# A graph layer's attention contracts gathered source rows (at most 512 a head) in place of all 1354

## The reference

```python
def _gat_head(h, node_adj, edge_adj, W, a):       # three heads, summed
    hW = h @ W
    hp = (node_adj > 0).astype(hW.dtype) @ hW
    hm = (node_adj < 0).astype(hW.dtype) @ hW
    e_plus = leaky_relu(concatenate([hp, hm], axis=1) @ a, ALPHA)[:, 0]
    e_minus = leaky_relu(concatenate([hm, hp], axis=1) @ a, ALPHA)[:, 0]
    att = where(edge_adj > 0, e_plus[None, :], NEG_INF)
    att = where(edge_adj < 0, e_minus[None, :], att)
    att = softmax(att, axis=1)
    return att * edge_adj @ hW

node_support = node_adj_norm @ h                   # the diagonal is taken out
edge_output = _gru_cell(node_support, h, ...)
node_output = _gru_cell(edge_support, h, ...)      # edge_support: the mean of the three heads
return de[:, None] * edge_output + dn[:, None] * node_output
```

## Time and profile before

| | |
|---|---|
| median of 3 runs | 535.05 us (533.65 to 535.43) |
| span of the profiled execution, first to last instruction | 520.2 us |
| median less span | 14.85 us |
| PE busy | 450.7 us, 87% of the span |
| DVE busy | 342.4 us, 66% |
| ACT busy | 239.3 us, 46% |
| POOL busy | 69.8 us, 13% |
| mean granted clock of PE, as a share of 2.4 GHz | 0.960 |

### The profile page before, as it was taken

How to read it: one execution, slowest core, us unless ns; L and a number is a source line. 1 busy time by engine, 2 the same in 40 slices (tenths; PEclk the granted TensorE clock), 3 DMA queues, 4 the chain that set the end, 5 groups by cost and what they waited for, 6 DMA issues and landing times.

```text
span 520.2 us, 6589 instructions
## 1 busy us (share of the span) xinstructions
PE 450.7 (87%) x1892; PEld 268.2 (52%) x1892; DVE 342.4 (66%) x753; ACT 239.3 (46%) x390; POOL 69.8 (13%) x115
## 2 busy tenths in 40 slices
PE   4588598977698998998979999999988878999996
PEld 2533454544355664454644444444444556787875
DVE  0997979787648772225773887787577655744572
ACT  4987789577777552104134031222213036644441
POOL 5000000000011000000000000100600502564442
PEclk9679788989989999999999999999989999999999
DMA  8889500000000000000000000530100111122422
GB/s 282 275 265 372 238 0 0 0 1 1 0 2 1 0 2 0 1 0 3 1 0 0 1 0 31 184 111 20 45 6 1 48 43 44 53 68 64 123 68 84
DMA packets 27006, 31.70 MB, mean 61 GB/s; under 512 B 3490, under 2 KB 20591, under 8 KB 26967
## 3 DMA queue, kind: packets, MB, share of 16 engines
q1 hardware_dynamic: 25111, 27.71, 16.8%
q0 software_dynamic: 1856, 3.51, 2.0%
HBM read 19.44 MB, written 11.77 MB: 60 GB/s over the span
## 4 chain that ended last, share of the span: by engine, by line
PE 53%; DVE 25%; ACT 11%; issue 9%; POOL 1%; DVEq 0%; POOLq 0%; ACTq 0%
PE bank L1340 9%; PE bank L1149 4%; PE bank L1422 4%; PE bank L1406 4%; PE bank L1288 4%; PE bank L1407 3%; DVE pr_ring L2074 3%; PE bank L1110 2%; DVE y_units L1551 2%; PE bank L1329 2%; DVE y_units L1562 2%; PE bank L999 2%; PE bank L1413 2%; DVE hr_ring L1877 2%; DVE t_units L1557 2%
## 5 line engine op out<-in xcount | busy, mean ns | idle before, releaser
L1340 PE MATMUL bank<-pr_ring,hW 128*128 128x512 f32 (+3 forms) x198 | 94.1, 560 | 6.1 <-DVE pr_ring L2074 5.4
L2074 DVE SCALAR_TENSOR_TENSOR pr_ring<-adjT,regR,bank 128x512 f32<-128x512 f32 (+3 forms) x99 | 64.7, 680 | 35.5 <-PE bank L1329 34.0
L1340 PEld LDWEIGHTS bank<-pr_ring,hW 128*128 128x128 f32 (+1 forms) x198 | 34.4, 193 | 35.3 <-DVE pr_ring L2074 18.4
L999 PE MATMUL bank<-y_units,msg 128*128 128x512 f32 (+3 forms) x66 | 34.4, 652 | 15.1 <-DVE y_units L1572 15.0
L1110 PE MATMUL bank<-hr_ring,W2s 128*128 128x512 f32 (+1 forms) x96 | 45.3, 560 | 0.0
L1877 DVE TENSOR_TENSOR hr_ring<-hr_ring,bank 128x512 f32<-128x512 f32 (+1 forms) x48 | 29.5, 619 | 20.9 <-ACT hr_ring L796 14.9
L585 POOL DMA_INDIRECT yg<-pr_ring,goes x32 | 31.2, 976 | 50.9 <-DVE pr_ring L2113 49.0
L796 ACT ACTIVATE hr_ring<-bank,b1c 128x512 f32<-128x512 f32 (+1 forms) x48 | 29.8, 628 | 15.7 <-PE bank L972 15.7
L970 PE MATMUL bank<-zhi,W1hi 128*128 128x512 f32 (+1 forms) x48 | 35.1, 731 | 0.3 <-DVE zlo L1546 0.3
L2125 DVE TENSOR_TENSOR hbuf<-hbuf,bank 128x341 f32<-128x341 f32 x36 | 18.3, 508 | 23.9 <-PE bank L1407 21.1
L579 POOL DMA_INDIRECT xg<-rowx,slot x22 | 22.3, 1013 | 69.6 <-DVE slot L1684 63.5
(11 more groups left out here) (321 smaller groups left out, 889.9 us busy)
## 6 DMA issues: line engine op xcount, KB each, us to landing
xg<-zeros SPq DMA_DIRECT2D x1, 3575.0 KB
xg<-zeros SPq DMA_DIRECT2D x1, 3055.0 KB
wall<-in_w SPq DMA_DIRECT2D x2, 1364.0 KB
adjT<-in_adjT SPq DMA_DIRECT2D x1, 2560.0 KB
xblk<-xg SPq DMA_DIRECT2D x36, 65.0 KB
adjT<-in_adjT SPq DMA_DIRECT2D x1, 1650.0 KB
adjT<-in_adjT SPq DMA_DIRECT2D x3, 512.0 KB, 5.9
adjT<-in_adjT SPq DMA_DIRECT2D x1, 1024.0 KB
```

The source lines that it names most:

```text
L999: mm = nc.tensor.matmul(B_GNN[:, 0:w], msg[0:r, j, :], y_units[0:r, g % RINGY, i, 0:w], start=(j == 0), stop=(j == T - 1))
L1340: nc.tensor.matmul(B_ACC[:, 0:w], hW[0:r, j, k * P:(k + 1) * P], ring[0:r, 0:w], start=(k == 0 and j == 0), stop=(k == K - 1 and j == T - ...
L2074: nc.vector.scalar_tensor_tensor(out=pr_ring[0:r, 4 + p % R_RING, 0:w], in0=adjT[0:r, j, cols(c)], scalar=g_col[0:r, j, k:k + 1], in1=B_F[ ...
```

## The change

For each head, a source is needed if one of its neighbours (as a destination) has its top bucket at most one bucket above the source's own. The new code finds these sources, numbers them, and makes the loop run over four gathered tiles of 128 sources a head, in place of eleven tiles.

- `onehot_turned` turns the one-hot bucket rows. `reaches` multiplies, for each destination tile, the buckets in reach with the natural adjacency (`nat`, bf16), 33 matmuls in all, and DVE's `reached` masks the sum. `needed`, `needs`, `slots`, `numbered`, `placed`, `payload` and `listed` turn that into up to 512 slots a head and, for each slot, the source's bucket, its factor and its row number (`slot_row`, semaphore `row_set`).
- POOL then issues 36 indirect DMAs, one for each chunk, head and slot tile, from five new DRAM tables. The three tables `near` hold the 512 columns of chunk 0 and the 128 of `hW` of that head; `far1` and `far2` hold the columns of chunks 1 and 2. SP writes them earlier from `adjT` and `hW`, and writes zeros over their diagonals, one element at a time. `nat` is loaded by POOL with a cast, 7.3 MB read.
- The loop has 36 steps (`STEPS`); `numerator` waits for the gathered tiles (`fetched0` to `fetched11`). `spread` now has 12 transposes in all instead of 33.
- The branch on `flag` moves to just ahead of the loop, since it also covers a head that needs over 512 sources. With it, all the edge GRU's tasks (`gates`, `mid`, `new`, `blend`, `add` with n = 0) move out of the loop, ahead of it, where `gates(0, c)` waits for `add(0, c-1)` (`x_edge`).
- The side tasks left get new places in the 36 steps; those of chunk 1's routing stand behind the last step.

With the reference's inputs the three heads need 253, 304 and 421 sources by a count made from the reference's formulas, so the loop and not the general path runs.

```diff
 MAIN_PE = {
-    (0, 0): [("spread", 3)], (0, 1): [("spread", 4)], ...
-    (7, 0): [("var", 3, 1)], (7, 4): [("logits", 4)], (7, 5): [("ztok", 1)], (7, 7): [("prefix", 1)]}
+    1: [("turned", 3)], 3: [("turned", 4)], 5: [("turned", 5)], 7: [("turned", 6)], 9: [("turned", 7)], 11: [("turned", 8)],
+    13: [("gates", 1, 0)], 16: [("mid", 1, 0)], 21: [("mean", 3, 0)], 24: [("var", 3, 0)], 25: [("gates", 1, 1)], 27: [("logits", 3)], 28: [("ztok", 0)],
+    29: [("mid", 1, 1)], 31: [("prefix", 0)], 35: [("mean", 3, 1), ("var", 3, 1), ("logits", 4), ("ztok", 1), ("prefix", 1)]}
...
@@ sync
+            for c in range(C):
+                sp.wait_ge(s[f"adjT_in{c}"], 32)
+                for table in near_d if c == 0 else [far_d[c]]:
+                    sp.dma_start(table[0:full, 0:width(c)].rearrange("(t p) n -> p t n", p=P), adjT[:, 0:T - 1, cols(c)]).then_inc(s["edges_out"], 16)
...
@@ gpsimd
+            pool.wait_ge(s["y_mm"], TILES0)
+            pool.dma_start(nat[:, 0:T - 1, :], adj_d[0:full, :].rearrange("(t p) n -> p t n", p=P)).then_inc(s["nat_in"], 16)
...
+            for c in range(C):
+                for k in range(K):
+                    if c == 0:
+                        at(pool, "row_set", k + 1)
+                    for n in range(SLOTS):
+                        fetch(c, k, n)
...
@@ vector
+            def placed(k):
+                link(nc.vector.tensor_tensor(pay24[:, k, :, :]..., mask4[:, k, :, :]..., pay6[:, :, k, :]..., ALU.mult))
+                nc.vector.tensor_tensor(slot_hot[:, k, :, :], slot_mod[:, :, k]..., upto[:, :]..., ALU.is_equal).then_inc(s["slothot_set"], 1)
...
             def numerator(p):
-                h, j = divmod(p, T)
+                h, n = divmod(p, SLOTS)
...
+                if h == 0:
+                    at(dve, f"fetched{n}", 16)
+                elif n == 0:
+                    at(dve, f"fetched{3 + h}", 16 * SLOTS)
...
+            blend(0, 1)
+            add(0, 1)
+            overflow()
+            bucket_drop(2)
+            mid(0, 2)
+            at(dve, "neg_ps", 2)
+            nc.vector.tensor_scalar(flag[0:1, 1:2], B_SIDE[0:1, 0:1], 0.0, None, ALU.is_gt).then_inc(s["flag_set"], 1)
+            blend(0, 2)
+            add(0, 2)
+            at(dve, "flag_set", 2)
+            general = dve.value_load(flag[0:1, 1:2], min_val=0, max_val=1)
```

More of the change, by code:

```diff
@@ L135 @@
 MAIN_PE = {
[L136 to L139, removed]
@@ L150 @@
-MAIN_ACT = [
[L151 to L155, removed]
+    1: [("turned", 3)], 3: [("turned", 4)], 5: [("turned", 5)], 7: [("turned", 6)], 9: [("turned", 7)], 11: [("turned", 8)],
@@ new lines @@
+    13: [("gates", 1, 0)], 16: [("mid", 1, 0)], 21: [("mean", 3, 0)], 24: [("var", 3, 0)], 25: [("gates", 1, 1)], 27: [("logits", 3)], 28: [("ztok", 0)],
+    29: [("mid", 1, 1)], 31: [("prefix", 0)], 35: [("mean", 3, 1), ("var", 3, 1), ("logits", 4), ("ztok", 1), ("prefix", 1)]}
+MAIN_DVE = {
+    0: [("share", 2)], 1: [("rest", 2, 0)], 2: [("rest", 2, 1)], 16: [("mid", 1, 0)], 18: [("blend", 1, 0), ("add", 1, 0)], 22: [("center", 3, 0)],
+    25: [("scale", 3, 0)], 27: [("scores", 3), ("ranks", 3), ("picks", 3)], 29: [("weights", 3), ("mid", 1, 1)], 31: [("blend", 1, 1), ("add", 1, 1), ("slots", 3)],
+    35: [("center", 3, 1), ("scale", 3, 1), ("scores", 4), ("ranks", 4), ("picks", 4), ("weights", 4), ("slots", 4), ("starts", 0), ("list", 0)]}
@@ L156 @@
+MAIN_ACT = [
+    ("part", 2, 0), ("turned", 3), ("part", 2, 1), ("part", 2, 2), ("turned", 4), ("turned", 5), ("turned", 6), ("turned", 7), ("turned", 8),
+    ("support", 0), ("gates", 1, 0), ("new", 1, 0), ("table",), ("center", 3, 0), ("support", 1), ("var", 3, 0), ("rank", 3), ("table", "tanh"),
+    ("ztok", 0), ("gates", 1, 1), ("new", 1, 1), ("table",), ("center", 3, 1), ("var", 3, 1), ("rank", 4), ("ztok", 1)]
 PRE_ACT = [("support", 2), ("gates", 1, 2)]
@@ L810, in _ @@
                 nc.scalar.copy(nsT[:, cols(c)], B_NS[c][:, 0:width(c)]).then_inc(s["ns_set"], 1)
+            for c in range(C):
+                at(act, "hot_ps", 1)
+                nc.scalar.copy(onehotT[0:K * BUCKETS, cols(c)], B_REACH[c][0:K * BUCKETS, 0:width(c)]).then_inc(s["hot_set"], 1)
             def gates(n, c):
@@ L924, in experts @@
                 hidden_turned(NB - 1)
+            gates(0, 0)
+            bucket_factor(0)
+            for i in range(PARTS):
+                share_part(0, i)
+            new(0, 0)
+            bucket_factor(1)
+            gates(0, 1)
+            for i in range(PARTS):
+                share_part(1, i)
+            new(0, 1)
+            for i in range(K):
+                share_copy(i)
+            for k in range(K):
+                spread_copy(k)
+            gates(0, 2)
+            bucket_factor(2)
+            new(0, 2)
             act.wait_ge(s["flag_set"], 2)
@@ new lines, in reaches @@
+            def reaches(i):
+                r = rows(i)
+                at(pe, "nat_in", 32)
+                at(pe, "reach_set", i // 4 + 1)
+                if i == 0:
+                    take_side("reached", C)
+                at(pe, "hot_set", C)
+                for c in range(C):
+                    mm = nc.tensor.matmul(B_REACH[c][0:K * BUCKETS, 0:width(c)], reach[0:r, i, :], nat[0:r, i, cols(c)],
+                                          start=(i == 0), stop=(i == T - 1))
+                    if i == T - 1:
+                        mm.then_inc(s["reach_ps"], 1)
@@ L1500, in _ @@
             with pe.If(general == 1):
-                for c in range(C):
-                    gates(0, c)
-                    mid(0, c)
+                at(pe, "spread_set", K)
+                at(pe, "reload", 16 * 2 * (C + K))
                 for c in range(C):
@@ L2186, in _ @@
                 dve.sem_inc(s["b_free"], 1)
-                for c in range(C):
-                    mid(0, c)
-                    blend(0, c)
-                    add(0, c)
+                at(dve, "reload", 16 * 2 * (C + K))
                 for h in range(C * K):
```

515 lines of the change are left out of this document (353 added, 162 removed).

## The result

The changed kernel takes 560.93 us (median of 4 runs, 558.29 to 561.78), the kernel before 534.35 (4 runs, 531.83 to 535.43). The ratio is 1.052, 95% interval 1.046 to 1.058. The forecast was 530 with a range up to 545, so it missed in sign and in size.

The account below looks back on a forecast made before the run. The prediction took PE to bound the attention loop. Its parts, 315 + 42.5 + 52 + 105.6, gave a span of 515.1 us; with 14.85 from span to median the forecast was 530 us, range 513 to 545.

Parts of the forecast that it names:

- Part 1: Up to the first attend, from 265.1 us to some 315, with DVE setting the pace late: a cost of 50 us.
- Part 2: First attend to `es_set` of chunk 1, 42.5 us in place of 105, with gathers hidden: a gain of 62.5 us.
- the 3 us of stalls: Early loop: `share(2)` and two `rest` queue on DVE behind numerators 0, 1 and 2, two waiting for ACT: 3 us.
- The 4 us of stalls: Loop steps 16 and 18: `mid`, `blend` and `add` of (1,0) on DVE outlast a ring of three: 4 us.
- Part 3: From `es_set(1)` to the first expert block, 52 us in place of 46.0, with worse interleaving: a cost of 6 us.
- Part 4: Experts: 104.1 us as before, plus 1.5 for PE's half rate behind an idle stretch, 105.6 in all.
- The 14.85 us between median and span: Whole kernel: the gap by which the median exceeded the profiled span, kept unchanged and added to the sum.
- The gathers are late: Slower rival, 12%: from 2.2 us a gather, `fetched` 1 to 11 and POOL's routing constants come late; at 3.0, end near 547.
- Half clock: Slower rival, 20%: PE at half rate over part 1's last 15 us and part 3's 24, longer hand-offs: 11 us, 541.
- The chains overlap better: Faster rival, 25%: part 1 costs 43, part 2's stalls are 4 not 7, part 3 is unchanged: 16 us lower, 514.
- shared port pair: Gathers on POOL: a DVE operation in two-port mode blocks GpSimd's descriptor writes, so gathers would be spread out; no size given.
- The sum's gain of 5.1 us: Whole kernel: the four parts sum to 515.1 us, 5.1 us under the span before.

Follow-up runs that it names:

- far_paced: The changed kernel without the general path, each group of four far gathers held until the attention loop is about eight steps ahead of it: 541.52 us, ratio 1.013.
- c_before: The kernel before, unchanged, run and profiled again for its own span in several executions: 531.82 us, ratio 0.998.

## Why the prediction was wrong

**The sum came out at 515.1 of span, and 558.4 is 43.3 more.** Term by term:

- *Part 1, 315.* Measured 315.9. Right (its last terms add up to 313.0 and not 313.5, which changes nothing), with `gates(0,2)` behind `add` of chunk 1 and a clock of 0.63 in the last 26 us. The first product's signal is already 2 us late, but DVE is busy nearly as long and waits 0.4 for it.
- *Part 2, 42.5.* **This is the step that failed**: measured 71.0. 22.2 us are the standstill. "The 36 gathers ... cost nothing up to some 2.2 us each" looked only at who waits for a gather's data. No numerator in the changed kernel waits for one, though a gather lands after 4.0 to 4.6 us (the three whose landings are all on record) and not 2.3; their price is on PE's signals, and it is high just because they are issued as fast as POOL can. The other 6.3 us were mis-sized, nearly all at half clock. The first five steps take 12.9 us besides the standstill, where the forecast has some 9.0 (five at 1.07, the 3 us of stalls, two turned shares): a pair of attends takes 2.0 to 2.1 us in them and not 1.02. The last five steps with `mean` take 8.4 in place of some 6.2, the first pair at 2.07 again, behind a wait of 2.4 us. The 4 us of stalls ahead of them were right (1.4 and 2.4).
- *Part 3, 52.* Measured 53.4. Right: `mean(3,1)` 29.7 us behind `es_set(1)`, forecast 28.
- *Part 4, 105.6.* Measured 118.1. 7.5 us are not the change's: before has them, in all but the shown execution. The 6.5 more than before again are, within 0.2, three things: 2.1 in the first block, at half clock (9.2 us from its transpose to the first turned hidden copy, 7.1 before), 1.5 in catching up behind the late signals, and 3.1 at the end, where SP waits 3.3 us for PE's sequencer, 0.2 before. Forecast for all of it: 1.5.
- *The 14.85 us between median and span.* "Which I keep" was wrong: in the runs made here a time is 1.7 to 2.3 us over its own span. The 14.85 mixed a short execution with a median of ordinary ones. That error (12.7 us too much) made up for that of part 4 (12.5 too little), by luck. The profile of before could not tell that it was unusual; that time and span were so far apart was the hint.

**The rivals.** "The gathers are late" had the right sign and 547, but the wrong mechanism and threshold: gathers at 1.25 us each, the fast case that I gave no cost, did it. "Half clock" was partly so, some 8 us (6 in the loop, 2 in the first block). "The chains overlap better" didn't happen. The Trainium skill's shared port pair ("SBUF — State Buffer") would have shown as gathers stretched by DVE. Of the 24 far gathers two are followed later than the usual 1.25 us, those at 313.28 (by 1.54) and 316.07 (by 1.38), both beside a DVE that works without a break. So this trace shows at most 0.4 us that could be it.

**What is left of the change.** Beside before again, far_paced starts its loop 53.5 us later, saves 54.9 in it, and loses 5.4 ahead of the blocks and 6.4 in them. Without the standstill it comes out 1.3% slower. The sum's gain of 5.1 us rested on the loop at 42.5 and the experts at 105.6.

**What stays open.** Why an indirect DMA each 1.25 us holds PE's signals, or its work, back: the trace records when a signal rose, not what held it. Where between 1.25 and 2.5 us it begins was not tried, nor how long a burst must be; why twelve in a row did nothing in three runs and nine scatters in a row held signals back by up to 8 us in c_before is not explained. Nor is it shown that the signals are late in an execution that is not traced: every one timed here has a span and a clock on record, and the trace itself loses records in these stretches. Why the shown execution of before, with the same six scatters 1.27 us apart, has no late signal is not explained either; every other profile here has them.

## What to carry to other kernels

A long burst of indirect DMAs that nobody waits for can stop the kernel: pace it to the work that uses it, and look for waits put down to "remote" while GpSimd sends. Cost a background transfer by what its issue does to the other engines as well as by when its data are needed. Before a median is set against a profile, compare the profiled execution's own time with its span; when they are 15 us apart, it is another kernel's profile for the purpose of a sum, and its stretches must be taken again.

## What the hardware showed that was not expected

- Signals of TensorE came up to 22 us late while GpSimd sent 36 indirect DMAs in a row, one each 1.25 us, with 4 bytes a row as with 2 KB in 24 of them, and with 16 rows (17 us late) as with 128. At one in 2.5 us none was late, and in three runs none behind twelve in a row at 1.25 us. A DMA share of 0.96 over 10 us, mostly plain loads, made them no later than in far_paced, and 160 memsets on GpSimd did nothing to them.
- In such a stretch in the changed kernel's experts the signals came 2.15 us apart, in c_before 1.4 to 2.2. The Trainium skill, "TensorE: Matmul & The Clock Gate", on the per-tile semaphore tail, gives some 26 ns an increment for increments that queue up; the 2.15 us of this trace are 80 times that.
- A gather of 128 rows of 2560 bytes takes GpSimd 0.95 us, with 0.30 to the next, and lands 4.0 to 4.6 us after its issue (three near gathers; of the others the trace has not all the landing records).
